# Linear attention and FFN over 128 tiles on one core: the output projection, the FFN and what follows them one slot later, another order on TensorE, and loads cut by columns

## The reference

```python
q = exp(split_heads(x @ Wq.T + bq)); k = exp(split_heads(x @ Wk.T + bk)); v = split_heads(x @ Wv.T + bv)
kv = cumsum(k[:, :, :, None] * v[:, :, None, :], axis=1)      # along the sequence
num = einsum('zsD,zsDd->zsd', q, kv); den = sum(q * cumsum(k, axis=1), axis=-1, keepdims=True)
x = layernorm(x + (merge_heads(num / den) @ Wo.T + bo))
out = layernorm(x + tanh(x @ weight @ aux_weight1 @ aux_weight2 + bias))
```

## Time and profile before

| | us |
|---|---|
| median of 3 runs | 2304.31 |
| the profiled execution | 2303.22 |
| its span, first to last instruction | 2301.4 |
| TensorE busy (share of the span) | 2241.9 (97%) |
| VectorE busy | 1617.2 (70%) |
| GpSimd busy | 1294.2 (56%) |
| ScalarE busy | 1012.3 (44%) |

### The profile page before, as it was taken

The page is one execution under the profiler, slowest core; times in us unless marked ns, Lnnn a source line. Parts: engine busy times, 40 slices in busy tenths (PEclk is TensorE's granted clock), DMA queues, the critical chain, the costliest instruction groups (busy, mean ns, idle before and its releaser), DMA issues.

```text
span 2301.4 us, 77308 instructions
## 1 busy us (share of the span) xinstructions
PE 2241.9 (97%) x27752; PEld 1829.6 (80%) x27752; DVE 1617.2 (70%) x2456; ACT 1012.3 (44%) x1695; POOL 1294.2 (56%) x1797
## 2 busy tenths in 40 slices
PE   7999999999999999999999999999999999999985
PEld 6778888888888888888888888888888888887864
DVE  5576776776776776776776776776776776767674
ACT  4344444444444444444444444444444444444432
POOL 1356556556556556556556555555555555555554
PEclk9999999999999999999999999999999999999997
DMA  7133333333333333333333333333333333333221
GB/s 183 57 110 111 104 111 111 103 111 112 103 110 112 103 111 111 102 111 112 102 109 114 103 110 112 103 111 111 104 112 109 105 108 112 106 103 108 71 70 56
DMA packets 294574, 243.17 MB, mean 106 GB/s; under 512 B 33424, under 2 KB 225936, under 8 KB 294288
## 3 DMA queue, kind: packets, MB, share of 16 engines
q1 hardware_dynamic: 293136, 236.59, 33.3%
q10 hardware_dynamic: 1152, 2.10, 0.3%
HBM read 139.99 MB, written 98.57 MB: 104 GB/s over the span
## 4 chain that ended last, share of the span: by engine, by line
PE 95%; DVE 2%; issue 1%; SPq 1%; ACT 1%; DMA 1%; POOL 0%; POOLq 0%; DVEq 0%; ACTq 0%
PE SC L326 26%; PE SC L328 25%; PE SC L327 25%; PE SC L417 6%; PE ND L393 5%; PE ND L384 3%; PE ND L380 2%; PE ND L428 2%; DVE o L803 1%; DMA WK<-wT 0%; SPq L253 0%; ACT A L648 0%; DVE WK L816 0%; SPq L241 0%; PE ND L327 0%
## 5 line engine op out<-in xcount | busy, mean ns | idle before, releaser
L916 POOL TENSOR_SCALAR_AFFINE_SELECT A<-A 128x512 f32<-128x512 f32 x512 | 331.8, 682 | 321.1 <-ACT A L648 321.0
L803 DVE RECIPROCAL o<-ND 128x512 f32<-128x512 f32 x128 | 427.8, 3342 | 0.1
L857 DVE TENSOR_TENSOR xres<-SC,xres 128x512 f32<-128x512 f32 x128 | 88.5, 692 | 431.8 <-PE SC L328 431.6
L910 POOL TENSOR_TENSOR oL<-o,oH 128x512 fp32r<-128x512 f32 x128 | 166.4, 1300 | 327.0 <-ACT oH L627 327.0
L638 ACT ACTIVATE WK<-xres,shift,rstd 128x512 f32<-128x512 f32 x128 | 104.1, 814 | 531.7 <-POOL shift L951 531.7
L648 ACT ACTIVATE A<-SC 128x512 f32<-128x512 f32 x512 | 264.7, 603 | 43.3 <-PE SC L417 43.3
L326 PE MATMUL SC<-xTH,WqH 128*128 128x512 f32 x512 | 210.8, 412 | 9.5 <-ACT QT L598 3.7
L326 PE MATMUL SC<-WfH,x1H 128*128 128x512 f32 x512 | 201.0, 393 | 14.4 <-issue 7.9
L816 DVE TENSOR_TENSOR_SCAN WK<-ones,k,KT 128x128 f32<-128x128 f32 x512 | 207.5, 467 | 7.1 <-PE ND L380 6.8
L326 PE MATMUL SC<-WoH,oH 128*128 128x512 f32 x512 | 201.1, 393 | 11.3 <-issue 9.3
L598 ACT ACTIVATE QT<-SC,bcol 128x512 f32<-128x512 f32 x128 | 88.4, 690 | 270.4 <-PE SC L328 270.4
(11 more groups left out here) (103 smaller groups left out, 4983.3 us busy)
## 6 DMA issues: line engine op xcount, KB each, us to landing
xres<-x SPq DMA_DIRECT2D x128, 256.0 KB, 2.6
x_rows<-WK SPq DMA_DIRECT2D x128, 256.0 KB, 3.1
WK<-x_rows SPq DMA_DIRECT2D x512, 64.0 KB, 2.0
out<-WK SPq DMA_DIRECT2D x128, 256.0 KB, 2.0
xin<-x SPq DMA_DIRECT2D x504, 64.0 KB, 1.9
k_rows<-WK SPq DMA_DIRECT2D x120, 256.0 KB, 2.0
WK<-k_rows SPq DMA_DIRECT2D x480, 64.0 KB, 2.2
A<-a1T ACTq DMA_DIRECT2D x4, 256.0 KB, 5.4
```

The lines of the kernel that those rows point to most:

```text
L803: nc.vector.reciprocal(o[:, :, :], den_ps).then_inc(recip_ready, 1)
L857: nc.vector.tensor_tensor(r, oproj_ps, r, ALU.add).then_inc(r_ready, 1)
L910: nc.gpsimd.tensor_tensor(oL[:, :, :], o[:, :, :], oH[:, :, :].bitcast(F32), ALU.subtract).then_inc(ol_ready, 1)
L916: last = nc.gpsimd.affine_select(out=A[:, k % 2, j, :, :], in_=A[:, k % 2, j, :, :], compare_op=ALU.is_ge, fill=0.0, base=0, pattern=[[0, ...
```

## The change

O of tile k-2 and F of tile k-3 are done in slot k, and the operations that follow them (r, its statistics, x1, x1s, x1H, x1L, z, tanh, output) are a slot later too; oH and oL are still made in the slot after the tile's attention. There are four slots behind the last tile instead of three. TensorE's order in a slot is small, Q, O, V, K, F; where there is no more Q, it is small, V, O, F. Every load in four pieces now has pieces of 128 columns (or of one block of 512) for all 128 partitions. At the start SyncE's queue also loads the two FFN matrices, between the x tiles, and ScalarE's queue loads Wq and Wk; on ScalarE and VectorE the split of w moves behind the split of the product of the other two, and on ScalarE behind the first `keep_k`. The aligned parts are K (0) and F (48), with 12 positions a step. In the diff, parts that only rename or move lines are left out.

```diff
-    x_b = x.rearrange("b (i t p) (a f) -> b i a p t f", t=P // HD, p=HD, a=HG)
+    x_b = x.rearrange("b (i t p) (a f) -> b i t a p f", t=P // HD, p=HD, a=HG)
 
     k_rows = nc.dram_tensor("k_rows", [P, D], F32).ap()
     x1_rows = nc.dram_tensor("x1_rows", [P, D], F32).ap()
-    k_blocks = k_rows.rearrange("(a p) (t c) -> t p a c", a=HG, t=HG)
-    x1_blocks = x1_rows.rearrange("(t p) (a f) -> a p t f", t=HG, a=HG)
+    k_blocks = k_rows.rearrange("(a p) (t c) -> a t p c", a=HG, t=HG)
+    x1_blocks = x1_rows.rearrange("(t p) (a f) -> t a p f", t=HG, a=HG)
...
+        def load_blocks(engine, tile, a, semaphore):
+
+            rows = a.rearrange("(a f p) n -> f a p n", a=HG, p=HD)
+            for f in range(NK):
+                engine.dma_start(tile[:, f, :], rows[f]).then_inc(semaphore, 16)
...
+                for t in range(HG):
+                    sp.dma_start(x_buffer(c, n)[:, t * P:(t + 1) * P],
+                                 x_b[n % B, c.it + n // B, t]).then_inc(xin_loaded[n % B], 16)
...
+                if c.updates_state(k - 1):
+                    n = k - 1
+                    wait_before(sp, (k_turned, c.count(n + 1)))
+                    sp.dma_start(k_rows, KS).then_inc(k_stored[n % B], 16)
+                if c.exists(k - 1):
+                    n = k - 1
+                    if c.static() and c.it * B + n == 0:
+                        sp.wait_ge(c_done, 1)
+                    wait_before(sp, (x1_ready, c.count(n - 1)))
+                    sp.dma_start(xres[:, n % 2, :], x_t[n % B, c.it + n // B]).then_inc(xres_loaded[n % B], 16)
+                if c.updates_state(k - 1):
+                    n = k - 1
+                    wait_before(sp, (k_stored[n % B], c.dma_count(n)), (state_done, c.count(n)))
+                    for a in range(HG):
+                        sp.dma_start(Ktok[:, a * P:(a + 1) * P], k_blocks[a]).then_inc(ktok_loaded[n % B], 16)
+                if c.exists(k + 9):
+                    n = k + 9
+
+                    wait_before(sp, (xl_ready, c.count(n - 1)))
+                    load_x(c, n)
                 if c.exists(k - 2):
                     n = k - 2
                     wait_before(sp, (x1_ready, c.count(n + 1)))
                     sp.dma_start(x1_rows, x1[:, n % 2, :]).then_inc(x1_stored[n % B], 16)
 
                     wait_before(sp, (x1_stored[n % B], c.dma_count(n)), (x1l_ready, c.count(n)))
+                    for t in range(HG):
+                        sp.dma_start(x1s[:, t * P:(t + 1) * P], x1_blocks[t]).then_inc(x1s_loaded[n % B], 16)
+                if c.exists(k - 4):
+                    n = k - 4
                     wait_before(sp, (out_ready, c.count(n + 1)))
                     sp.dma_start(out_t[n % B, c.it + n // B], y[:, n % 2, :]).then_inc(out_stored[n % B], 16)
...
+            def load_aux(f):
+                sp.dma_start(a1T_raw[:, f, :], a1T.rearrange("(k p) n -> k p n", p=P)[f]).then_inc(aux_loaded[f], 16)
+                sp.dma_start(a2_raw[:, f, :], a2.rearrange("(k p) n -> k p n", p=P)[f]).then_inc(aux_loaded[f], 16)
+
             first = Chunk(0)
+            load_aux(0)
             load_x(first, 0)
+            load_aux(1)
             load_x(first, 1)
-            load_by_block(wq_raw, wqT, wq_loaded)
+            load_aux(2)
             load_x(first, 2)
+            load_aux(3)
             load_x(first, 3)
-            load_by_block(wk_raw, wkT, wk_loaded)
             load_biases()
             sp.dma_start(w_raw, w.rearrange("(k p) n -> p k n", p=P)).then_inc(w_loaded, 16)
             sp.wait_ge(xl_ready, 1)
             load_x(first, 4)
             sp.wait_ge(xl_ready, 2)
             load_x(first, 5)
-            load_by_block(wv_raw, wvT, wv_loaded)
+            load_blocks(sp, wv_raw, wvT, wv_loaded)
             sp.wait_ge(auxl_ready, 2 * NK)
-            load_by_block(wo_raw, woT, wo_loaded)
+            load_blocks(sp, wo_raw, woT, wo_loaded)
...
-                        pe.addr_align(256, offset=place + 10 * k, max_nops=255)
+                        pe.addr_align(256, offset=place + 12 * k, max_nops=255)
...
-                    wait(pe, z_ready, c.count(k - 2))
+                    wait(pe, z_ready, c.count(k - 3))
                     wait(pe, k_ready, c.count(k + 4))
                     wait(pe, v_ready, c.count(k))
-                    wait(pe, r_ready, c.count(k - 1))
+                    wait(pe, r_ready, c.count(k - 2))
...
+            k_place, f_place = 0, 48
...
+            def keys(c, k):
+                align(c, k_place)
...
+            def output_projection(c, k):
+
+                n = k - 2
+                if not c.exists(n - 1):
+                    pe.wait_ge(woh_ready, 1)
+                    pe.wait_ge(wol_ready, 1)
+                wait(pe, oh_ready, c.count(n + 1))
+                wait(pe, ol_ready, c.count(n + 1))
+
+                if c.exists(k):
+                    wait(pe, scores_out[3], c.count(k + 1))
+                wait(pe, r_ready, c.count(n))
+                three_pass(oproj_ps, lambda f: oH[:, f, :], lambda f: oL[:, f, :],
+                           lambda f: WoH[:, f, :], lambda f: WoL[:, f, :]).then_inc(oproj_done, 1)
...
+            def feed_forward(c, k):
+
+                n = k - 3
+                align(c, f_place)
+                wait(pe, x1h_ready, c.count(n + 1))
+                wait(pe, x1l_ready, c.count(n + 1))
...
+            def first_half(c, k):
+                small(c, k)
+                if c.exists(k + 4):
+                    queries(c, k)
+                    if c.exists(k - 2):
+                        output_projection(c, k)
+                if c.exists(k):
+                    values(c, k)
+                    if not c.exists(k + 1):
+                        denominators(c, k)
+                        attend(c, k)
+
+            def second_half(c, k):
+                if c.exists(k + 4):
+                    keys(c, k)
+                elif c.exists(k - 2):
+                    output_projection(c, k)
+                if c.exists(k - 3):
+                    feed_forward(c, k)
...
+                first_half(*place(t))
+                second_half(*place(t))
+
+            first_half(Chunk(1), 0)
             with nc.Fori(1, NI - 2, engines=(pe.engine,), hint_back_edge=True, head_slot={pe.engine: 232}) as it:
                 c = Chunk(it, pe)
                 for k in range(B):
-                    values_output_ffn(c, k)
-                    small(c, k + 1)
-                    queries_and_keys(c, k + 1)
-            for t in range(NT - 2 * B, NT + 2):
-                c, k = Chunk(t // B), t % B
-                if t > NT - 2 * B:
-                    small(c, k)
-                    queries_and_keys(c, k)
-                values_output_ffn(c, k)
+                    second_half(c, k)
+                    first_half(c, k + 1)
+            second_half(*place(NT - 2 * B))
+            for t in range(NT - 2 * B + 1, NT + 3):
+                first_half(*place(t))
+                second_half(*place(t))
...
+                    copy_v(c, k)
+                if c.exists(k - 3):
+                    n = k - 3
+                    wait(act, x1_turned, c.count(n + 1))
+                    wait(act, ffn_done, c.count(n))
                     nc.scalar.activation(x1H[:, :, :].rearrange("p g (t q) -> p g t q", q=HD),
                                          x1s[:, :].rearrange("p (t g q) -> p g t q", t=HG, q=HD),
                                          ACT.Copy).then_inc(x1h_ready, 1)
+                if c.exists(k - 1):
+                    n = k - 1
+                    wait(act, o_ready, c.count(n + 1))
+                    wait(act, oproj_done, c.count(n))
+                    nc.scalar.activation(oH[:, :, :], o[:, :, :], ACT.Copy).then_inc(oh_ready, 1)
+                if att and proj:
+                    copy_v(c, k)
+                if c.exists(k - 2):
+                    n = k - 2
+                    wait(act, shift1_ready, c.count(n + 1))
+                    wait(act, y_ready, c.count(n - 1))
+                    nc.scalar.activation(x1[:, n % 2, :], xres[:, n % 2, :], ACT.Identity, bias=shift[:, 0:1],
+                                         scale=rstd[:, 0:1]).then_inc(x1_ready, 1)
+                if c.exists(k + 8):
+                    split_x(c, k)
                 if proj:
                     keep_k(c, k)
                 if fin:
+                    n = k - 4
                     wait(act, shift2_ready, c.count(n + 1))
                     nc.scalar.activation(y[:, n % 2, :], y[:, n % 2, :], ACT.Identity, bias=shift[:, 1:2],
                                          scale=rstd[:, 1:2]).then_inc(out_ready, 1)
...
             split_aux(0)
+            load_blocks(act, wq_raw, wqT, wq_loaded)
             split_aux(1)
+            load_blocks(act, wk_raw, wkT, wk_loaded)
+            split_x(*place(-8))
             split_aux(2)
+            split_x(*place(-7))
             split_aux(3)
+            split_x(*place(-6))
```

(70 more changed lines are left out.)

298 lines of the change are left out of this document (73 added, 225 removed).

## The result

The changed kernel takes 2345.6 us (median of 4 runs, 2343.08 to 2350.68) against 2304.48 for the kernel before (4 runs, 2303.34 to 2304.90): 1.0182 times as long, interval 1.0164 to 1.0200. The forecast was 2286.9, in a range of 2279 to 2298. The profiled execution has a span of 2343.5 us, 42.1 more than before.

A forecast was written before the change was run, and what follows sets the result against it. TensorE's own work was taken to pace the loop, leaving gains only outside it: -8.1 - 8.6 - 1.6 - 10.0 + 10.9 = -17.4 from 2303.22, so 2285.8, plus 1.1 for the median: 2286.9 us, range 2279 to 2298.

The forecast's parts named there:

- The start: Up to the first scores: earlier `keep_q`, less slow clock and faster loads save 3.7 + 3.0 + 2.1 less 0.7, so -8.1 us.
- The term of the clock: In the start: without the idle time TensorE's clock stays higher; half of 6.0 us lost to slow clock won back, 3.0.
- if the wf product waits for w: In the start: condition for the low end of the saving, 4.6 us, together with no load being faster.
- The exchange of queues alone gives nothing.: At the start: spreading transfers over issuing engines saves only issue time, so swapping queues was counted as no gain.
- The first slots: First eight slots: one O and one F leave, and waits for a score copy and oL go, -8.6 us.
- The loop: Steady slots: TensorE's own work paces them and `keep_k` keeps 2 us of room, so 0, allowing about 2 us.
- Behind the loop: After the loop: TensorE's one wait of 1.6 us is covered by the room for oL and x1L, -1.6 us.
- The last slots with scores: Slots 124 to 126: O no longer waits for oL of the same slot; three slots of 13.0 us, -10 us.
- The end: Behind the last scores: one more tile to finish as its own chain, 11.4 less 0.5, so +10.9 us.
- Rival 1: The start does not win, loads late by what they gained; 4.6 us or less, down to 0; 2290.5 to 2295; chance 0.17.
- Rival 2: Last slots stay at 15 to 16 us through x1's round trip and the end costs 14; 2298; chance 0.1.
- Rival 3: In the loop `keep_k` slips and TensorE stops ahead of every score; half a microsecond gives 2343; chance 0.09.

The follow-up runs named there:

- e4: The kernel before with only the new pieces for all 128 partitions, nothing else of the change: 2344.76 us, 1.0183 of before.
- e8: Changed kernel with 128-partition pieces reading DRAM rows in natural order (other bytes per piece, output not the reference's): 2296.80 us, 0.9966 of before.
- e11: Changed kernel, same bytes per piece, the memory side's two outer dimensions exchanged (32 outside, 4 inside; output differs): 2296.54 us, 0.9968 of before.
- e1: Changed kernel with every load in the old pieces of 32 partitions; slots, order and queues as changed: 2301.52 us, 0.9995 of before.
- e5: e1 with the start's old queues (FFN matrices from ScalarE, Wq and Wk from SyncE), new order of splits kept: 2296.78 us, 0.9965 of before.
- e7: e5 with VectorE's normalise of the last tile moved behind r and the statistics of tile 125: 2290.75 us, 0.9941 of before.
- e10: e7 plus O of tile 125 ahead of tile 127's denominators and values, and attention weights laid out for natural-row 128-partition pieces: 2285.65 us, 0.9906 of before.

## Why the prediction was wrong

**The step that failed: "The start".** It took the rate "while pieces for all partitions moved" from the stretch at 314 GB/s, gave it to every piece for all partitions, and so had the first 5.2 MB come 3.3 us sooner. What moved there was mostly the FFN matrices (0.53 of 0.67 MB from 6.5 to 8.5 us), read in natural rows, with x pieces of 32 partitions between them. The pieces of the change have the same partitions but a memory side with 4 outermost, and move at 98 GB/s with a share of 0.27, so on a quarter of the engines (e4, e8, e11). The rate 209 that the change gave up was the better one. The Trainium skill's rule quoted with e11 would have given it, by both sides of one transfer; I weighed other sections of the Trainium skill, on ports and on issuing engines, and not this one. The first scores are 40.5 us later than forecast. By kernels this divides as follows: 29.6 pieces (98.49 against 68.91 in e1), 7.7 exchange of queues (e1 against e5), 3.2 what e5 is later than the forecast of 58.

**The 3.2 in "The start".** The waits among its three terms came: 3.7 and 2.1 less 0.7 would put Q of tile 1 at 27.4; in e5 it starts at 27.75 in place of 32.50. The term of the clock, 3.0, did not arrive as time. From there to the end of the product with w e5 needs 19.1 us, the kernel before 19.2: Q takes 3.47 in place of 5.26, and the 1.8 so won are lost again in the wait of 1.60 for w's low part, since w's split is now late. The text named this bound ("if the wf product waits for w") and put it at the low end instead of into the sum.

**"The exchange of queues alone gives nothing."** Shown wrong for pieces of 32 partitions (7.7 us); with faster ones it is open. What counts in e1 is the place of each transfer in the one order of arrival, and the first things needed were moved back in it.

**"The first slots"** (-8.6): -8.4 in all kernels with the new order. Right, by its own terms: the waits for score copies in these slots fell from 2.7 to 1.0, and the one of 1.3 for oL is gone.

**"The loop" and "Behind the loop"** (0 and -1.6): -3.3. By the starts of the scores it is -0.9 from tile 8 to 112 (1793.8 to 1792.9) and -2.5 from 112 to 120 (141.5 to 139.0), where three slots of 18.3, 17.8 and 19.3 became one of 18.2. The room for `keep_k` is there. Right, and what is left over, 1.7, is within the allowance of 2; over the kernels with the new order the whole stretch varies from 1930.6 to 1933.6.

**"The last slots with scores"** (-10): the mechanism was right, -9.2 in e1 with slots of 13.0, 13.2 and 13.5. With the new pieces the transposes of x1s come late, the last two slots are 14.9 and 18.4, and only -2.6 is left. "A few tenths longer" was the condition set there; the round trip from the first issue of x1s to its transpose is 5.7 us at the end, against 3.4 in e1 (2256.96 to 2260.40).

**"The end"** (+10.9): +24.1. One part is again the pieces, 6.1 (74.30 against 68.20 in e1): each F comes 13.5 to 14.1 behind the one before it, against 10.8 to 11.7 in e1. The other is a wait that I did not count, +18.0 in e1 in place of +10.9: normalise of the last tile behind oL of tile 126, with r of 125 queued behind it. Taking it out gives 6.6 back (e7), close to the whole of the 7.1 missed. I followed the chain of each tile, and not what stands in VectorE's list between them.

**Together**, the misses by section are 40.5 + 0.2 - 1.7 + 7.4 + 13.2 = 59.6 us, and the span is 42.1 + 17.4 = 59.5 above the forecast's.

**The rivals.** Rival 1 named the right place and bounded the loss at 0; what it lacked is a rate below the one of before. Rival 2's place, x1's round trip, was right too, for a reason it did not have. Rival 3, which carried the chance of slower, did not happen; that its 2343 lies near the 2345.6 measured is an accident, as the loop lost nothing. The 0.08 for slower came from one mechanism in the loop, and none of the rivals asked whether the new transfers could be slower than the old.

## What to carry to other kernels

When loads are cut anew, write down both sides of one transfer, outermost dimension first, and take its rate only from a row whose transfer has the same outermost sizes; the same number of partitions is not enough. A DMA share near a simple fraction (here 0.27) with issues stretched to microseconds is a sign that few engines carry the transfers. Exchanging two dimensions raises the rate but brings the rows to other partitions; laying the data out in memory for it (e10) keeps the tile. Where work is pushed a slot later, walk each engine's list at the end of the run too: a buffer that has two slots of room in the loop can be held by an instruction that now comes behind the last tile.

## What the runs showed of the hardware

- The same bytes, with the same runs and the same number of transfers, moved at 98 GB/s with a memory side of 4 x 32 rows and at 304 to 384 with 32 x 4 (changed kernel and e11).
- With the slow transfers the issuing engine is held up: 12.58 us for four issues, the longest 7.4, in place of 0.44 each; in e11 0.47 to 0.71 each.
- VectorE's sum of two SBUF operands took 0.65 us alone and 1.18 to 1.47 when it began within a GpSimd pass, and ended 0.54 behind that pass (kernel before, e7).
- TensorE's granted clock was 0.56 from 18 to 28 us, where it had no matmul, and 0.79 from 66 to 98 us, where it stood for 13.3 us once; a late load costs a second time there.
- The store of x1 landed in 2.0 us (3.1 before), at its new place in the slot; the cause is open.
